# Moving the subtraction that forms the low parts of the next batch's tokens from VectorE to GpSimd, in a fused attention and int8 linear kernel

## The reference

```python
q = (X @ Wq), k = (X @ Wk), v = (X @ Wv)      # 16 heads of q, 8 of k and v, 64 wide
q, k = rope(q), rope(k)
att = 50 * tanh(q @ k.T * 256**-0.5 / 50)     # causal
y = softmax(att) @ v
x = layernorm(x + y @ Wo)
q8, in_scale = per_token_quant_int8(x)
x = layernorm(x + float16((q8 @ weight.T) * in_scale * w_scale + bias))
```

## Time and profile before

| | |
|---|---|
| three runs | 1385.95, 1387.62, 1388.68 us; median 1387.62 |
| the profiled execution | 1386.44 us, its span from first to last instruction 1384.5 us |
| mean granted TensorE clock | 0.977 |
| busy, share of the span | PE 93%, PEld 68%, DVE 75%, ACT 65%, POOL 28% |

### The profile page before, as it was taken

One profiled execution on the slowest core, in us unless ns is written; L12 is line 12 of the kernel. 1 busy time (PEld: TensorE's weight loads), 2 busy tenths in 40 slices (PEclk: granted clock), 3 DMA queues, 4 the chain that ended last, 5 costly groups with the idle time before them and its releaser, 6 DMA issues.

```text
span 1384.5 us, 17005 instructions
## 1 busy us (share of the span) xinstructions
PE 1293.5 (93%) x5840; PEld 941.3 (68%) x5840; DVE 1034.7 (75%) x1307; ACT 894.8 (65%) x1016; POOL 382.7 (28%) x446
## 2 busy tenths in 40 slices
PE   6779999999989999999998999999999899999795
PEld 5657777667666777676765777767666677777563
DVE  4568888882668888886477888888556888888555
ACT  5267787772466877865356777686436677879454
POOL 2232111111671111111274111111147321111266
PEclk9989999999999999999999999999999999999897
DMA  8966446385723454729451645455763254453631
GB/s 325 284 210 164 92 130 145 103 240 155 180 74 81 130 140 89 204 54 264 147 152 58 141 99 134 94 173 144 223 164 92 66 152 92 115 111 114 168 108 53
DMA packets 109505, 196.16 MB, mean 142 GB/s; under 512 B 19302, under 2 KB 61804, under 8 KB 101484
## 3 DMA queue, kind: packets, MB, share of 16 engines
q1 hardware_dynamic: 104812, 186.69, 50.6%
q10 hardware_dynamic: 4608, 8.39, 1.6%
HBM read 89.39 MB, written 38.54 MB: 92 GB/s over the span
## 4 chain that ended last, share of the span: by engine, by line
PE 70%; DVE 8%; POOL 8%; DMA 6%; issue 4%; ACT 2%; SPq 2%; POOLq 0%; DVEq 0%; ACTq 0%
PE ps L751 24%; PE ps L670 17%; PE ps L725 15%; PE ps L692 6%; PE ps L793 5%; POOL y_lo L1369 3%; POOL f L1387 2%; POOL probs L1389 2%; DMA y_scratch<-sums 1%; DMA qk<-work_r 1%; POOL rstd L1378 1%; DVE prob_hi L1167 1%; DVE stats L1247 1%; DMA bias<-L_ffn_bias 1%; PE ps L813 1%
## 5 line engine op out<-in xcount | busy, mean ns | idle before, releaser
L751 PE MATMUL ps<-prob_hi,v 128*65 128x512 f32 (+3 forms) x1280 | 414.5, 374 | 14.4 <-DVE prob_lo L1171 14.4
L938 ACT ACTIVATE probs<-ps 128x1024 f32<-128x1024 f32 x288 | 293.5, 1019 | 164.6 <-PE ps L725 150.7
L1171 DVE TENSOR_TENSOR prob_lo<-probs,prob_hi 128x1024 fp32r<-128x1024 f32 x288 | 361.1, 1254 | 9.8
L1363 POOL TENSOR_SCALAR_AFFINE_SELECT probs<-probs 128x256 f32<-128x256 f32 (+1 forms) x192 | 151.6, 797 | 768.0 <-ACT probs L943 768.0
L725 PE MATMUL ps<-qk 128*128 128x512 f32 (+1 forms) x1280 | 317.1, 374 | 16.0 <-DMA qk<-work_r 7.5
L943 ACT ACTIVATE probs<-probs 128x1024 f32<-128x1024 f32 x288 | 305.6, 1061 | 8.6
L670 PE MATMUL ps<-xT,w_ring 128*128 128x512 f32 x1152 | 289.9, 395 | 6.2 <-DVE xT L1094 5.8
L725 PEld LDWEIGHTS ps<-qk 128*128 128x128 f32 x1280 | 227.2, 191 | 76.6 <-DMA qk<-work_r 7.9
L1167 DVE CAST prob_hi<-probs 128x1024 fp32r<-128x1024 f32 x288 | 202.0, 701 | 94.6 <-POOL probs L1363 54.4
L670 PEld LDWEIGHTS ps<-xT,w_ring 128*128 128x128 f32 x1152 | 216.6, 190 | 53.1 <-DVE xT L1094 7.1
L751 PEld LDWEIGHTS ps<-prob_hi,v 128*65 128x65 f32 (+1 forms) x1280 | 172.2, 136 | 107.3 <-DVE prob_lo L1171 21.8
(11 more groups left out here) (81 smaller groups left out, 990.1 us busy)
## 6 DMA issues: line engine op xcount, KB each, us to landing
qk<-work_r SPq DMA_DIRECT2D x64, 512.0 KB, 8.7
qk<-work_r SPq DMA_DIRECT2D x256, 128.0 KB, 2.7
y_scratch<-sums SPq DMA_DIRECT2D x128, 130.0 KB
wo<-wo_scratch SPq DMA_DIRECT2D x8, 2048.0 KB, 8.3
y_raw<-y_scratch SPq DMA_DIRECT2D x64, 256.0 KB, 4.3
w_ring<-w_scratch SPq DMA_DIRECT2D x15, 1024.0 KB, 7.0
x_raw<-X_T SPq DMA_DIRECT2D x16, 512.0 KB, 6.7
x_in<-X SPq DMA_DIRECT2D x32, 256.0 KB, 4.3
```

The lines of the kernel that those rows point to most:

```text
L751: mm = nc.tensor.matmul(sums_ps[:, :, GQ - w:GQ], v[:, kt, v0:v0 + width], p[:, at, col:col + REP * w].rearrange("p (h q) -> p h q", h=REP ...
L938: nc.scalar.activation(probs[:, prob_place(g), :], scores[:, g % 2, :], ACT.Tanh, scale=SCORE_SCALE / SOFTCAP).then_inc(capped, 1)
L1171: nc.vector.tensor_tensor(prob_lo[:, prob_place(g), :], probs[:, prob_place(g), :], prob_hi[:, hi_place(g), :].bitcast(F32), ALU.subtract) ...
L1363: nc.gpsimd.affine_select(out=diag, in_=diag, compare_op=ALU.is_ge, fill=0.0, base=0, pattern=[[0, n], [1, P]], channel_multiplier=-1).the ...
```

## The change

VectorE's loop loses its call of `split_x`; its own four for the first batch stay. GpSimd gets a `split_x` of the same text, called at the same steps of its own loop, behind that step's mask. Tiles, shapes, semaphores and their counts are the same.

```diff
@@ VectorE, the main loop @@
                         if at := chunk_at(b, u, s, turns(u, 6, 11, 15)):
                             rope_low(*at)
-                        if more and (part := part_at(u, s)) is not None:
-                            split_x(b + 1, part)
@@ GpSimd @@
+            def split_x(b, u):
+                pool.wait_ge(xT_hi, parts_upto(b, u))
+                cols = slice(u * XW, (u + 1) * XW)
+                nc.gpsimd.tensor_tensor(xT[:, 1, :, cols], x_raw[:, :, cols],
+                                        xT[:, 0, :, cols].bitcast(F32), ALU.subtract).then_inc(xT_lo, 1)
@@ GpSimd, the main loop @@
                         if not at_end(b, u, s):
                             mask(b, g)
+                        if b + 1 < B and (part := part_at(u, s)) is not None:
+                            split_x(b + 1, part)
                         if b == 0 and u == 0 and 1 <= s < 5:
                             split_wo(s - 1)
```

## The result

The changed kernel takes 1401.93 us (median of 7 runs, 1397.49 to 1406.78); the kernel before, run beside it, 1389.45 (7 runs). The ratio is 1.0085, 95% interval 1.0062 to 1.0108: slower by 12 us, between 9 and 15. Both kernels scatter by some 5 us around their medians, so seams are compared within traces and totals by ratios.

The account below looks back on a forecast made before the run. TensorE, busy 93% of the span, was taken as the bound, with no slack for time lost at the seams. Turns 15.6 + clock 3.4 = 19.0 us, added to the median 1387.62, gave 1406.6; range 1397 to 1414.

Parts of the forecast that it names:

- seams: End of unit 2 and start of unit 3 of batches 0, 1 and 2, where four moved subtractions each stand.
- the turns: At each seam GpSimd and VectorE alternate whole instructions; projection starts 5.2 us later, 15.6 us for three; forecast's chance 0.80.
- the clock: TensorE's granted clock dips behind the first two seams as well, 2 x 1.7 = 3.4 us; bounds 0 and 8.5.
- The bound that booked 0.1 us more for each hand-over: High bound of the turns: 13 hand-overs each cost 0.1 us more, 6.5 a seam, 19.5 us for three.
- TensorE's waits: At the seam: two waits for `prob_lo` of about 4 and 2 us, about 2.3 us for the tokens, no other changed.
- the row alone, 0.94 of 14 us: Profile row behind the third seam: mean clock 0.94, read as 3.4 us at half clock, costing about 1.7 us.
- Rival A: GpSimd's subtractions run beside VectorE's `prob_lo`; only later masks and the last split delay the seams: +5.3, 1392.9; chance 0.09.
- Rival B: Seam loss given back in waits before the next value projection: 15.6 - 8.4 = 7.2, 1394.8; chance 0.06.
- C: Faster: VectorE's relief removes the short `prob_lo` waits at the seams, at most 3.3 us off, 1384.3; chance 0.02.
- D: No difference to measure, since the edit hits nothing that waits; chance 0.03.

Follow-up runs that it names:

- spare subtractions: Kernel before plus one unread 128x768 subtraction on GpSimd at each of the twelve seam places, VectorE keeping its own: 1.0163, 22.6 us slower.
- the spare subtractions elsewhere: Kernel before plus the same twelve unread GpSimd subtractions, at steps 1, 3, 6 and 7 of unit 2, ahead of the seam: ratio 1.0009.

## Why the prediction held, point by point

The direction, the mechanism and the range held: 1406.6 was forecast with 1397 to 1414, 1401.9 measured; 19.0 us of loss forecast, about 12 measured. Of the two terms of the sum the one for the turns was 2.2 us too high, and the one for the clock, 3.4 us, didn't appear. In the traces the loss up to the last value projection is 13.4 us at the seams and 0.6 between; by the medians the whole is 12.5.

**The turns, right.** The forecast length of a seam was 17.0 us of exclusive work; 16.1 to 16.3 were measured, so 15.6 us for three seams became 13.4. At the first seam the instructions have the order forecast, except that GpSimd's first subtraction was issued 0.06 us ahead of the rotation, so that each of GpSimd's first two came one place earlier, which left the sum as it was. The single turn was booked too high: a subtraction on GpSimd holds the other engine for 2.2 to 2.3 us, not 2.35 (255.73 to 257.94 at the last part), and a cast takes 0.55 (249.48 to 250.03), not 0.65. By these the sum is 4 x 1.15 + 4 x 2.25 + 3 x 0.55 + 3 x 0.35 = 16.3. At the second seam not all went by turns: its last subtraction, 595.97 to 598.32, took 2.35 us with nothing ahead of it, and the length was 16.26 all the same. The bound that booked 0.1 us more for each hand-over was on the wrong side.

**TensorE's waits, right in sum and wrong in pieces.** One wait of 3.8 us for `prob_lo` 15 came as forecast (4). The second (2) didn't: TensorE came back from the first at half clock, its weighing and scoring took until 253.4, and `prob_lo` 16 was done at 253.36. The wait for the tokens is 2.1 (2.3 forecast), and 2.5 and 1.5 at the other seams.

**The clock, wrong.** I expected one more slow stretch behind each of the first two seams, worth 3.4 us. A slow stretch came at all three, but inside the seam, behind the wait for `prob_lo`; behind the start of the projection there is one at the first seam only. Granted clock of the changed kernel at the first seam (from:to, length, PE busy, clock; 1.00 is 2.4 GHz, 0.50 is 1.2 GHz):

```profile
249.00:253.00 4.00, 3.73 (x10) 0.57 0.87 206
253.00:257.00 4.00, 2.82 (x12) 1.00 0.56 232
258.00:262.00 4.00, 4.00 (x12) 0.68 0.00 0
```

The first of them lies where TensorE has a wait ahead anyway, so it lengthens matmuls and shortens that wait: TensorE still waits 2.1 us for the tokens behind it. The second costs time. From the projection's start to the wait before the next value projection TensorE needs 54.1 us where the clock stays at 1.00 and it waits for nothing. The kernel before took 54.1, 54.1 and 57.4 us (the slow stretch of the earlier trace rows and two waits of 0.5 us lie in the last), the changed one 55.7, 54.1 and 54.1. So in place of 3.4 us more, this part became 1.7 us shorter. With the wait before the value projection included, the three stretches are 174.0 us before and 174.6 after. As for the size of a slow stretch: the row alone, 0.94 of 14 us, is a loss of 0.8 us; the 1.7 come only with the part of the stretch that lies ahead of 924 us (0.59 from 922 to 924).

**Rival A, refuted.** `prob_lo` took 3.30 us at the first seam, and spare subtractions that relieve nobody cost 22.6 us. The reading of the Trainium skill's "Advanced Engine Details and Errata", section VectorE Performance Modes, under which only two-port instructions collide, doesn't fit these rows; that of "SBUF — State Buffer", section Who interferes with whom, by which a VectorE instruction with two SBUF inputs collides with a GpSimd instruction that reads SBUF but not with one that only writes, agrees with 1.22 us under memsets and 3.30 under subtractions.

**Rival B, refuted.** The waits before the value projection would have had to shrink by 8.4 us in all. They didn't. TensorE's waits over the whole span, the kernel before, then the changed one:

```profile
PE ps L692 <- issue: 8.4, 3, 3.6
```

```profile
PE ps L692 <- issue: 10.8, 3, 4.3
```

They grew by 2.4 us (3.6, 2.4 and 2.4 before; 3.2, 4.3 and 3.3 after), where the prediction had no other wait changing. Why is open, and it may be scatter: their sum is 11.1 us in the run with the spare subtractions elsewhere, whose seams didn't move.

**Rivals C and D** ended with the sign. C's own condition, part 3 done by 254.01 of the first seam, failed by 4.4 us, counted from the rotation's issue (16.19 against 11.77).

## What to carry to other kernels

An idle GpSimd is no free VectorE. In these runs GpSimd's subtractions and masks took turns, by whole instructions, with VectorE's casts and two-input subtractions of tiles in SBUF. So a subtraction moved at a busy place costs VectorE the difference of the two durations (2.25 against 1.15 us) instead of saving it anything. Add up the exclusive work ahead of the result that the path waits for (rotation, casts, low parts, masks, splits: 17.0 us here, 16.2 measured), rather than each engine's own load; in a stretch with slack the same turns cost nothing that could be measured (1.0009, interval 0.9995 to 1.0022). And before work is moved because something waits for it, ask whether all of it is needed at that point: asking for two parts of four gained 9 to 10 us where the move lost 12.

## What the runs showed of the hardware beyond that

- With work queued on both sides the two engines alternated by whole instructions, and starts in the trace hide it: a GpSimd subtraction issued 0.06 us before VectorE's stretched that one from 1.22 to 3.44 us, while both are shown as running.
- Three memsets of 2.3 us together beside VectorE's two-input subtractions left these at 1.22 us, and lengthened casts of 0.69 us to 1.02 and 1.20.
- After a wait of 4.1 us TensorE's next eight matmuls took 3.4 to 3.8 us instead of 2.1; after waits of 3.5 to 3.8 us its matmuls went to half speed at once or within 1 us at all three seams of the changed kernel; after waits of 2.0 us its clock fell at one of three seams of the kernel before (the third), and with the spare subtractions elsewhere also at one of three, but the first (2.87 us for eight matmuls, then 2.12 and 2.11). After 3.25 us, at the first seam with spare subtractions, the eight took 2.12. So the length of the wait alone doesn't decide.
